# The last turns of a four-stage pipeline in another order, and the last expert layer in input halves

## The chip, the cores and the metric

The kernel runs on one core of a Trainium2 chip. The metric is the device time of one execution in microseconds; the time before is the median of three runs, 785.86 us (784.04 to 786.75). Engines are named as in the profile: PE (matrix products), DVE (vector), ACT (scalar, activation functions), POOL (GpSimd), SP (its queue issues the direct transfers).

## The reference, cut to what matters

Two layer blocks over x (2 x 2048 x 512, float32), each made of an attention-like part and a feed-forward part, all added to x after a layer norm without weights:

```python
x = x + relu(relu(relu(LN(x) @ Wq + bq) @ kp.T) / sqrt(512) + mask) @ vp)   # kp, vp from ctx (2 x 128 x 512)
x = x + dequant(quant6(LN(x))) @ dequant(quant6(W)).T + bias                # blocks of 32, FP6 grid
x = x + LN(x) @ W1.T + mean(ctx @ W2.T) + b                                 # the "mix"
n = LN(x)                                                                   # 16 experts, each takes the
p = softmax(n @ Wg + bg, over the sequence)                                 # 128 tokens of highest p
x[tokens] += (relu(relu(tok @ w1 + b1) @ w2 + b2) @ w3 + b3) * p            # for every expert
```

## The kernel before

Every product is made in three passes of float32r matmuls, from a high part and a rest (names with _h and _l): high x high, high x low, low x high. The high part is made by ACT (hi), the rest by DVE or POOL (lo).

**Phase 1** takes the 32 tiles of 128 tokens (N = 32) through four stages in a loop of turns k = 0 to 35 (LAST = N + 3). It is written out by hand, in one order for each engine; semaphores join them. In turn k a tile k is quantised and its result turned (t2), tile k-1 goes through the feed-forward product (ffn), tile k-2 is turned (t3) and mixed (mix), tile k-3 gets its second residual (x3), its norm for the experts (xn) and its gate logits (lt). Beside these, every fourth turn makes the scores of four tiles (scores; group 7, the last, in turn 27) and gathers logits (logit_rows, in turn 31 for group 6), and up to turn 26 each turn makes one chunk of q (q_chunk) for a later group. From turn 24 on no new tile of x is turned any more; tile 31 is quantised in turn 31, mixed in turn 33.

In an ordinary late turn PE does: t3(k-2), ffn(k-1), attend(k+1), t2(k), mix(k-2). t2(k) waits for xd(k), which POOL writes (L1625) after DVE's q (L1322). DVE does in order: x3(k-3) (L1293), which waits for the end of mix(k-3), its sums bn (L1116), the largest values amax, the scales xs, xrec, xrq, and q of tile k; then the rest of x2T (lo3), x2(k-1) (L1343) with sums, x1(k+1) (L1277) with sums, the rest of xdT (lo2). POOL has the reciprocal roots of the variances (rstd: three or so short operations each), the bias additions (L1611, L1631), xd, and the rests q_lo and s_lo. ACT has xc, the high parts, xn (L854), lt and lrow (L1044).

mix(k) accumulates its two halves of 256 output columns together in banks 6 and 7 and needs x3(k-1) read out of them. The scores go to bank 7 too. In turn 33 four matmuls whose result nobody reads (keep_warm) stand ahead of mix(31).

**Between the phases** all engines wait in phase1_over for the last transfers of phase 1. DVE then finds the 128 largest logits per expert (MAX8 and following), and tokens are gathered.

**Phase 2** runs 16 experts, PE without a pause. hidden(e, layer) makes the hidden layers in two pairs of column chunks, outputs(e) the last layer: for both batches b, 12 matmuls each, over the four input chunks d. It waits for the rests of all four (d_hlo 4e+4). After the last hidden layer twelve matmuls without use stand ahead of outputs(15); DVE scales the two results (y, L1504), and POOL adds each to the output by an indirect DMA (L1664).

```python
        pe.wait_ge(sm.a_h, 4 * E - 3)
        keep_warm(12, wh, ps_hid[0])
        outputs(E - 1)
```

Of the kernel before, what the change touches and what calls it, by code (L numbers as in the profile page):

```python
# [34 lines left out]
P = 128  # L35
# [10 lines left out]
def build(nc, io):  # L46
# [22 lines left out]
        a_xn1 a_xc a_xn4 a_hi1 a_hi2 a_hi3 a_q a_s a_l a_seg  # L69
# [5 lines left out]
    XR = 10  # L75
# [90 lines left out]
    xn4 = [place(f"xn4_{i}", [P, D]) for i in range(2)]  # L166
    top[0] = at_cd + 16 * 1024
# [287 lines left out]
    def _(pe):  # L455
# [59 lines left out]
        def scores(g):  # L515
# [4 lines left out]
            if g >= 1:  # L520
                pe.wait_ge(sm.a_s, g)
                pe.wait_ge(sm.a_l, GRP * g - 3)
                pe.wait_ge(sm.d_x3, GRP * g - 3)
            keys = slice(b * KEYS, (b + 1) * KEYS)
            three_passes(pe, ps_s[:, :], [(k_h[:, c, keys], k_l[:, c, keys], q_h[:, c, :], q_l[:, c, :])
# [22 lines left out]
        def mix(j):  # L548
# [27 lines left out]
            for d in range(1, C):  # L576
                low_tokens(d)
                low_weights(d)
                last = high(d)
            last.then_inc(sm.p_c, 1)  # L580

# [148 lines left out]
        for k in range(1, LAST + 1):  # L730
            if valid(k - 2):
                t3(k - 2)
            if valid(k - 1):
                ffn(k - 1)
# [8 lines left out]
            if scores_of(k) is not None:  # L743
                scores(scores_of(k))
# [6 lines left out]
            if valid(k + 1) and ahead(k):  # L751
                attend(k + 1)
# [74 lines left out]

        wh, _ = weights(0)
# [19 lines left out]
    def _(act):  # L848
# [58 lines left out]

        def norm1(j):
# [20 lines left out]
        def s_relu(g):  # L929
# [3 lines left out]
            act.activation(s32[:, :], ps_s[:, :], ACT.Relu, scale=float(D) ** -0.5).then_inc(sm.a_s, 1)  # L933
# [42 lines left out]
        for k in range(LAST + 1):  # L976
            j = k
            if valid(j):
                act.wait_ge(sm.d_st2, j + 1)
                act.wait_ge(sm.d_q8, j)  # L980
                act.activation(xc[:, :], x1[j % 2][:, :], ACT.Identity, bias=mv[1][:, j % 4, 0:1], scale=-1.0)\
                    .then_inc(sm.a_xc, 1)
            if k == 0:
                setup("wcn")
            j = k - 2
            if valid(j):
                act.wait_ge(sm.p_t3, j + 1)
                act.wait_ge(sm.p_c, max(0, j - 1))
                hi(sm.a_hi3, x2T[j % 2][0][:, :, :], in4(ps_ta))
            j = k - 3  # L990
            if valid(j):
# [4 lines left out]
                act.activation(four, both_halves[:, :, HALF:WIDE], ACT.Copy).then_inc(sm.a_l, 1)  # L996
# [11 lines left out]
            j = k - 3  # L1008
            if valid(j):
                if j >= 2:  # L1010
                    act.wait_ge(sem_xn4[j % 2], 16 * (j // 2))
                norm(3, j, x3[j % 2], xn4[j % 2], sm.a_xn4, sm.g_b4)
            g = scores_of(k)
            if g is not None:
# [23 lines left out]
            if g is not None:  # L1038
# [3 lines left out]
                if g >= 2:  # L1042
                    act.wait_ge(sem_seg[g % 2], 16 * (g // 2))
                act.activation(lrow[g % 2][:, :], ps_ta[0:E * GRP, 0:P], ACT.Identity, bias=bg[:, 0:1])\  # L1044
                    .then_inc(sm.a_seg, 1)

# [60 lines left out]
    def _(dve):  # L1107
# [165 lines left out]
        def first_residual(j):  # L1273
# [464 lines left out]
```

## Time and profile before

| | us |
|---|---|
| median of three runs | 785.86 |
| the profiled execution, its own time | 786.94 |
| its span, first to last instruction | 785.1 |
| turn 27 of phase 1 (from 355.4) | 14.4 |
| turns 28, 29 and 30 | 8.9 each |
| turn 31 | 10.9 |
| turns 32 and 33, to the last mix | 12.0 |
| from there to the first MAX8 | 6.3 |

The span is 1.8 us shorter than the execution's own time, which has what lies around it. Times in the trace are from the span's start. A row of the timeline gives an instruction's start and duration, and in brackets how long the engine had been idle before it and which instruction released it. Matmuls are pipelined: the starts tell their rate, the durations overlap.

### The profile page before, as it was taken

The numbers are of one execution on the slowest core, as the hardware profiler recorded it, in microseconds if no ns is written. First come the engines' busy times: TensorE is split into PE (matmuls) and PEld (weight loads), VectorE is DVE, ScalarE is ACT, GpSimd is POOL, SyncE is SP. The second block draws the span as 40 slices with busy tenths as digits, with TensorE's granted clock in tenths as the row PEclk, the third lists the DMA queues.
The fourth block names the chain that finished last, engine by engine and source line by source line (L and its number), as shares of the span: only waits on it lengthen the run. The fifth ranks groups of instructions, "written<-read, shape, count | busy, mean of one in ns | idle before, by whom it ended". The sixth has DMA issues, their size and how long they took to land.

```text
span 785.1 us, 12311 instructions
## 1 busy us (share of the span) xinstructions
PE 697.4 (89%) x4357; PEld 618.3 (79%) x4357; DVE 572.6 (73%) x1016; ACT 377.8 (48%) x554; POOL 433.3 (55%) x596
## 2 busy tenths in 40 slices
PE   6999999999999999998883007999999999999993
PEld 5766888888888888887672006999999999999992
DVE  5787689898888988777875984576666767677741
ACT  5754444544544444342322203656566666665640
POOL 2735788888888888886752603044444333334321
PEclk9999999999999999999997557999999999999998
DMA  8600122222212221111114244278888888777742
GB/s 312 230 28 14 42 95 67 88 66 92 69 56 96 81 83 50 61 54 43 54 56 156 74 167 119 97 225 243 241 245 236 233 243 239 237 219 218 221 64 34
DMA packets 54093, 103.04 MB, mean 131 GB/s; under 512 B 5392, under 2 KB 6672, under 8 KB 54032
## 3 DMA queue, kind: packets, MB, share of 16 engines
q1 hardware_dynamic: 46864, 85.47, 33.1%
q0 software_dynamic: 7168, 16.78, 9.6%
q8 instruction: 35, 0.57, 0.3%
q14 instruction: 26, 0.21, 0.1%
HBM read 76.68 MB, written 25.17 MB: 130 GB/s over the span
## 4 chain that ended last, share of the span: by engine, by line
PE 81%; DVE 10%; POOL 3%; issue 2%; DMA 1%; ACT 1%; SPq 0%; POOLq 0%; DVEq 0%; ACTq 0%
PE bank L250 45%; PE banks L250 13%; PE bank L257 7%; PE banks L560 4%; PE banks L566 4%; PE banks L570 2%; PE banks L571 2%; DVE pack L1384 1%; DVE left L1391 1%; DVE pos L1386 1%; DVE bn L1116 1%; POOL xd L1625 1%; DVE x L1293 1%; ACT xn L854 1%; DVE q L1322 1%
## 5 line engine op out<-in xcount | busy, mean ns | idle before, releaser
L1664 POOL DMA_INDIRECT out<-y,ids x32 | 76.1, 2379 | 173.6 <-DVE y L1504 169.0
L1128 DVE TENSOR_TENSOR w_l<-w_raw,w_h 128x2048 fp32r<-128x2048 f32 x45 | 103.0, 2289 | 31.3 <-ACT w_h L858 31.3
L1079 ACT ACTIVATE h<-bank,b 128x512 f32<-128x512 f32 x64 | 44.0, 687 | 107.4 <-PE bank L250 107.4
L1116 DVE BATCH_NORM_STATS2 bn<-x 128x6 f32<-128x512 f32 x128 | 88.1, 688 | 8.4 <-DMA x<-x 5.1
L858 ACT ACTIVATE w_h<-w_raw 128x2048 fp32r<-128x2048 f32 x48 | 90.6, 1924 | 5.4 <-DMA w_raw<-w 5.4
L1128 DVE TENSOR_TENSOR hT_l<-h,hT_h 128x512 fp32r<-128x512 f32 x64 | 44.2, 691 | 66.9 <-ACT hT_h L1085 66.9
L250 PE MATMUL bank<-hT_h,w_h 128*128 128x256 f32 x256 | 72.4, 283 | 0.0
L250 PE MATMUL bank<-hT_h,w_l 128*128 128x256 f32 x256 | 72.4, 283 | 0.0
L250 PE MATMUL bank<-tokT_l,w_h 128*128 128x256 f32 x256 | 72.4, 283 | 0.0
L250 PE MATMUL bank<-tokT_h,w_h 128*128 128x256 f32 x256 | 72.4, 283 | 0.0
L250 PE MATMUL bank<-hT_l,w_h 128*128 128x256 f32 x256 | 72.4, 283 | 0.0
L250 PE MATMUL bank<-tokT_h,w_l 128*128 128x256 f32 x256 | 72.4, 283 | 0.0
L1540 POOL TENSOR_SCALAR rstd<-mean_var 128x1 f32<-128x1 f32 x122 | 29.2, 239 | 55.7 <-DVE mean_var L1121 51.7
L1653 POOL DMA_INDIRECT tok<-xn,ids x32 | 31.9, 998 | 47.0 <-DVE ids L1474 28.9
L250 PE MATMUL bank<-wf_h,xdT_h 128*128 128x512 f32 x128 | 53.0, 414 | 0.0
L250 PE MATMUL banks<-w_h,hT_h 128*128 128x512 f32 x128 | 51.2, 400 | 0.0
L250 PE MATMUL bank<-wf_h,xdT_l 128*128 128x512 f32 x128 | 50.3, 393 | 0.0
L250 PE MATMUL bank<-wf_l,xdT_h 128*128 128x512 f32 x128 | 50.0, 391 | 0.0
L250 PE MATMUL banks<-w_h,hT_l 128*128 128x512 f32 x128 | 49.9, 390 | 0.0
L250 PE MATMUL banks<-w_l,hT_h 128*128 128x512 f32 x128 | 49.8, 389 | 0.0
L250 PEld LDWEIGHTS bank<-hT_l,w_h 128*128 128x128 f32 x256 | 49.1, 192 | 0.6
L250 PEld LDWEIGHTS bank<-hT_h,w_h 128*128 128x128 f32 x256 | 49.1, 192 | 0.6
(244 smaller groups left out, 2159.2 us busy)
## 6 DMA issues: line engine op xcount, KB each, us to landing
w_raw<-w SPq DMA_DIRECT2D x48, 1024.0 KB, 6.3
x<-x SPq DMA_DIRECT2D x32, 256.0 KB, 2.8
out<-x SPq DMA_DIRECT2D x32, 256.0 KB, 2.0
xn<-xn SPq DMA_DIRECT2D x32, 256.0 KB, 2.0
mask<-mask_t SPq DMA_DIRECT2D x8, 256.0 KB, 3.1
stage<-wk SPq DMA_DIRECT2D x1, 1024.0 KB, 7.8
stage<-wq SPq DMA_DIRECT2D x2, 512.0 KB, 7.8
stage<-wf SPq DMA_DIRECT2D x1, 1024.0 KB, 10.8
```

Of the source, the lines that this page charges most:

```text
L250: last = pe.matmul(out, a, b, start=(n == 0), stop=(n == 3 * len(pairs) - 1))
L257: last = pe.transpose(bank[:, c * P:(c + 1) * P], src[:, c * P:(c + 1) * P], ident[:, :])
L560: last = pe.matmul(both_halves[:, a, 0:WIDE], xh[:, d, :], wc_h[:, d, a, :], start=(d == 0), stop=(d == C - 1))
L566: pe.matmul(both_halves[:, a, 0:HALF], xh[:, d, :], wc_l[:, d, a * HALF:(a + 1) * HALF], start=False, stop=False)
L570: pe.matmul(both_halves[:, 0, 0:WIDE], xl[:, d, :], wc_h[:, d, 0, :], start=False, stop=False)
L858: act.activation(dst, src, ACT.Copy).then_inc(sem, 1)
L1079: act.activation(h32[n % 2][:, :], ps_hid[n % 4][:, :], ACT.Relu, bias=bias)
L1116: dve.bn_stats(bn6[which][:, j % 2, :], src[:, :]).then_inc(sem_bn[which], 1)
L1128: dve.tensor_tensor(dst, src, hi_part, ALU.subtract).then_inc(sem, 1)
L1540: then(pool.tensor_scalar(r[:, 0:1], m[:, 1:2], LN_EPS, None, ALU.add))
L1653: pool.indirect_dma_start(out=tok[e % 2][:, b, :], out_offset=None, in_=io.xn4, in_offset=bass.IndirectOffsetOnAxis(ap=ids[:, r:r + 1], ax ...
L1664: pool.indirect_dma_start(out=out_rows, out_offset=bass.IndirectOffsetOnAxis(ap=ids[:, r:r + 1], axis=0), in_=y[e % 2][b][:, :], in_offset ...
```

## The change

Turns 25 to 35 are called drain turns.

- PE: attend(k+1) stands right behind t3 and ahead of ffn. The scores of group 7 stand at the head of turn 27, ahead of t3, and go to bank 2 (ps_q[0]), so that they do not wait for x3 and lt.
- DVE: where no scores stood in the turn before (quant_first: turns 25, 26, 27, 29, 30, 31), amax to q of tile k stand ahead of x3(k-3). x1(k+1) stands ahead of x2(k-1), with a third x1 buffer. The sums bn and their mean and variance for x3 are left out for tiles 22 to 29.
- ACT: for those tiles it makes the sums instead (sums4: an ACTIVATE Copy and an ACTIVATE Square of 128x512, each with an accumulator); xn of a tile stands a turn later, behind hi3. xn(31) stands behind the last lrow. SP's order is the same.
- POOL: xd and the bias addition stand at the head of the turn, the roots behind them; s_lo of group 7 stands ahead of the mix bias.
- t3(31) stands inside mix(30), after half of its matmuls. mix(31) makes its output halves one after the other in banks 2 and 3 (last_mix), and x3(31) is made in halves. The four idle matmuls ahead of it are gone.
- Phase 2: outputs(15) takes input chunks 0 and 1 of both batches first, then 2 and 3 (last_outputs); the twelve idle matmuls are gone.

```diff
+    SUMMED = range(N - 10, N - 2)
+    def drain(k):
+        return k >= N - 7
+    def scores_first(k):
+        return scores_of(k) is not None and drain(k)
+    def quant_first(k):
+        return drain(k) and scores_of(k - 1) is None
...
         for k in range(1, LAST + 1):
-            if valid(k - 2):
+            if scores_first(k):
+                scores(scores_of(k))
+            if valid(k - 2) and k - 2 != N - 1:
                 t3(k - 2)
+            if valid(k + 1) and ahead(k) and drain(k):
+                attend(k + 1)
             if valid(k - 1):
                 ffn(k - 1)
...
-            if valid(k - 2):
-                if k == LAST - 2:
-                    pe.wait_ge(sm.a_q, N)
-                    keep_warm(4, wq_h, ps_q[0])
+            if valid(k - 2) and k - 2 != N - 1:
                 mix(k - 2)
+            if k - 2 == N - 1:
+                last_mix()
...
+        def last_outputs():
+            e = E - 1
+            wh, wl = weights(when[(e, 2)])
+            for pair in range(2):
+                pe.wait_ge(sm.d_hlo, 4 * e + 3 + pair)
+                for b in range(B):
+                    if pair == 0:
+                        pe.wait_ge(sm.d_y, B * e + b - 1)
+                    t = slice(b * P, (b + 1) * P)
+                    for d in (2 * pair, 2 * pair + 1):
...
-        pe.wait_ge(sm.a_h, 4 * E - 3)
-        keep_warm(12, wh, ps_hid[0])
-        outputs(E - 1)
+        last_outputs()
...
+        def sums4(j):
+            m = mv[3][:, j % slots[3], :]
+            n = j - SUMMED.start
+            act.wait_ge(sm.a_st4, n)
+            act.activation(squares[:, :], x3[j % 2][:, :], ACT.Copy, scale=-1.0 / D, accum_out=m[:, 0:1])\
+                .then_inc(sm.a_sum, 1)
+            act.wait_ge(sm.a_sum, n + 1)
+            act.activation(squares[:, :], x3[j % 2][:, :], ACT.Square, bias=m[:, 0:1], accum_out=m[:, 1:2])\
+                .then_inc(sm.a_st4, 1)
...
         for k in range(LAST + 1):
+            if valid(k) and quant_first(k):
+                largest(k)
+                quantise(k)
+            if k - 2 == N - 1:
+                third_low(N - 1)
             j = k - 3
...
+            if ahead(k) and drain(k) and valid(k + 1):
+                first_residual(k + 1)
...
+            if drain(k):
+                if scores_first(k):
+                    s_lo(scores_of(k))
+                elif valid(k + 1):
+                    rstd_of(1, k + 1, sm.d_st2, sm.g_r2)
+                if valid(k - 2):
+                    mix_bias(k - 2)
+                if valid(k - 2) and k > N - 7:
+                    rstd_of(2, k - 2, sm.d_st3, sm.g_r3)
+                if valid(k - 3):
+                    rstd_of(3, k - 3, sm.d_st4, sm.g_r4)
+                if scores_first(k):
+                    rstd_of(1, k + 1, sm.d_st2, sm.g_r2)
```

The order on PE at the start of turn 27, before. The first row is the end of mix(24), x_1 is x2 of tile 25 (t3), the products with wf are ffn(26); twelve rows of ffn stand before the first product with kT.

```order
L560 MATMUL banks<-wc_wg_h,x2T_0h 128x288 x2
L257 MATMUL bank<-ident,x_1_125 128x128 x4
L250 MATMUL bank<-wf_h,xdT_h 128x512
L250 MATMUL bank<-wf_l,xdT_h 128x512
L250 MATMUL bank<-wf_h,xdT_l 128x512
```

The same place of the changed kernel, from the last three of the twelve score products:

```order
L252 MATMUL bank<-qT_h,kT_h 128x512
L252 MATMUL bank<-qT_l,kT_h 128x512
L252 MATMUL bank<-qT_h,kT_l 128x512
L259 MATMUL bank<-ident,x_1_125 128x128 x4
L252 MATMUL bank<-wf_h,xdT_h 128x512
L252 MATMUL bank<-wf_l,xdT_h 128x512
L252 MATMUL bank<-wf_h,xdT_l 128x512
```

The scores have moved from behind ffn to ahead of t3.

The order on DVE in turn 29, before; x_0_140 is x3 of tile 26, x_0_124 is x2 of tile 28.

```order
L1293 SCALAR_TENSOR_TENSOR x_0_140<-banks,rstd_all_54,x_0_124 128x512
L1116 BN_STATS bn_72<-x_0_140 128x6
L1307 TENSOR_REDUCE amax<-xc 128x16
L1121 BN_AGGR mean_var_68<-bn_72 128x2
L1317 TENSOR_SCALAR xs<-amax,rstd_74 128x16
L1320 RECIPROCAL xrec<-xs 128x16
L1321 TENSOR_SCALAR xrq<-xrec,rstd_74 128x16
L1322 TENSOR_TENSOR q_113<-xc,xrq 128x512
L1128 TENSOR_TENSOR x2T_1l<-bank,x2T_1h 128x512
L1343 TENSOR_TENSOR x_0_124<-bank,x_0_133 128x512
```

And the changed kernel in the same turn:

```order
L1384 TENSOR_REDUCE amax<-xc 128x16
L1394 TENSOR_SCALAR xs<-amax,rstd_74 128x16
L1397 RECIPROCAL xrec<-xs 128x16
L1398 TENSOR_SCALAR xrq<-xrec,rstd_74 128x16
L1399 TENSOR_TENSOR q_113<-xc,xrq 128x512
L1411 SCALAR_TENSOR_TENSOR x_0_140<-banks,rstd_all_54,x_0_124 128x512
L1225 TENSOR_TENSOR x2T_1l<-bank,x2T_1h 128x512
L1376 SCALAR_TENSOR_TENSOR x_0_133<-bank,x_97 128x512
L1213 BN_STATS bn_70<-x_0_133 128x6
L1218 BN_AGGR mean_var_66<-bn_70 128x2
L1495 TENSOR_TENSOR x_0_124<-bank,x_2_144 128x512
```

q no longer stands behind x3, the sums of x3 are gone, and x1(30) with its sums stands ahead of x2(28).

The order on PE from the end of mix(30) (x2T_0) over t3(31) to mix(31) (x2T_1), before:

```order
L560 MATMUL banks<-wc_wg_h,x2T_0h 128x288 x2
L257 MATMUL bank<-ident,x_1_125 128x128 x4
L459 MATMUL bank<-wq_h 128x512 x4
L560 MATMUL banks<-wc_wg_h,x2T_1h 128x288 x2
L566 MATMUL banks<-wc_l,x2T_1h 128x256 x2
```

And after:

```order
L594 MATMUL banks<-wc_wg_h,x2T_0h 128x288 x2
L259 MATMUL bank<-ident,x_1_125 128x128 x4
L604 MATMUL banks<-wc_wg_h,x2T_0l 128x288
L605 MATMUL banks<-wc_wg_h,x2T_0l 128x256
L600 MATMUL banks<-wc_l,x2T_0h 128x256 x2
L594 MATMUL banks<-wc_wg_h,x2T_0h 128x288 x2
L604 MATMUL banks<-wc_wg_h,x2T_0l 128x288
L605 MATMUL banks<-wc_wg_h,x2T_0l 128x256
L600 MATMUL banks<-wc_l,x2T_0h 128x256 x2
L594 MATMUL banks<-wc_wg_h,x2T_0h 128x288 x2
L628 MATMUL bank<-wc_wg_h,x2T_1h 128x288
L629 MATMUL bank<-wc_l,x2T_1h 128x256
```

t3(31) has moved in front of the second half of mix(30), and mix(31) follows with nothing between.

## Rows read from the trace of the kernel before

**Rows 1.** The page: granted TensorE clock in 40 slices of 19.6 us.

```profile
PEclk9999999999999999999997557999999999999998
```

**Rows 2.** Windows: us, busy time (instructions) of PE, PEld, DVE, ACT, POOL, clock, DMA.

```profile
355.50:370.00 14.50, 12.21 (x63) 10.59 (x62) 9.34 (x20) 3.70 (x7) 8.90 (x14) 0.88 0.11 40
370.00:378.90 8.90, 7.55 (x49) 6.58 (x48) 7.59 (x16) 2.85 (x5) 7.00 (x12) 1.00 0.16 59
396.70:407.60 10.90, 8.52 (x47) 7.62 (x46) 6.61 (x15) 2.37 (x5) 5.95 (x9) 0.84 0.14 52
407.60:419.40 11.80, 10.79 (x72) 9.54 (x70) 5.97 (x11) 3.06 (x6) 5.46 (x10) 1.00 0.24 89
419.40:425.70 6.30, 0.30 (x1) 0.11 (x1) 2.76 (x8) 1.29 (x3) 1.13 (x3) 0.79 0.24 88
```

**Rows 3.** Timeline of PE, turns 27 to 33: start, duration, what, idle before.

```profile
355.41 0.60 PE L257 MATMUL bank<-ident,x 128*128 128x128 f32 x4
...
364.35 0.50 PE L250 MATMUL bank<-v_h,s_h 128*128 128x512 f32 x1 [2.29 <-POOL s_l L1557]
...
369.81 0.60 PE L257 MATMUL bank<-ident,x 128*128 128x128 f32 x4
...
375.20 0.65 PE L257 MATMUL bank<-ident,xd 128*128 128x128 f32 x4 [1.35 <-POOL xd L1625]
...
378.70 0.49 PE L257 MATMUL bank<-ident,x 128*128 128x128 f32 x3
...
402.25 0.80 PE L257 MATMUL bank<-ident,xd 128*128 128x128 f32 x4 [2.38 <-POOL xd L1625]
...
407.42 0.60 PE L257 MATMUL bank<-ident,x 128*128 128x128 f32 x4
...
413.95 1.18 PE L459 MATMUL bank<-wq_h 128*128 128x512 f32 x4
416.13 0.53 PE L560 MATMUL banks<-wc_wg_h,x2T_1h 128*128 128x288 f32 x2 [1.00 <-DVE x2T_1l L1128]
```

**Rows 4.** Timeline of DVE in turn 28: x3 after mix, and q.

```profile
370.01 0.75 DVE L1293 SCALAR_TENSOR_TENSOR x<-banks,rstd_all,x 128x512 f32<-128x512 f32 x1 [2.94 <-PE banks L560]
...
372.94 0.69 DVE L1322 TENSOR_TENSOR q<-xc,xrq 128x512 fp8e4<-128x512 f32 x1
```

**Rows 5.** Timeline of POOL in turns 28 and 32.

```profile
373.23 0.54 POOL L1548 TENSOR_SCALAR rstd<-mean_var,rstd_all 128x1 f32<-128x1 f32 x1
373.73 0.29 POOL L1622 TENSOR_SCALAR xs<-xs 128x16 f32<-128x16 f32 x1
374.10 1.05 POOL L1625 TENSOR_TENSOR xd<-q,xs 128x512 f32<-128x512 fp8e4 x1
...
410.36 0.27 POOL L1548 TENSOR_SCALAR rstd<-mean_var,rstd_all 128x1 f32<-128x1 f32 x1
```

**Rows 6.** Timeline of ACT at the end of phase 1 and the top-k.

```profile
422.62 0.81 ACT L854 ACTIVATE xn<-x,rstd,rstd_all 128x512 f32<-128x512 f32 x1 [2.18 <-POOL rstd L1548]
423.34 0.35 ACT L1044 ACTIVATE lrow<-bank,bg_rows 64x128 f32<-64x128 f32 x1
426.75 0.72 ACT L1057 ACTIVATE exps<-seg_logits,negm 128x512 f32<-128x512 f32 x1 [3.06 <-DVE negm L1389]
427.38 0.19 ACT L1057 ACTIVATION_READ_ACCUMULATOR exps<-seg_logits,negm 128x1 f32 x1
```

**Rows 7.** Timeline of the last expert: PE, DVE, POOL.

```profile
764.60 2.91 PE L459 MATMUL bank<-w_h 128*128 128x512 f32 x12
767.35 0.39 PE L250 MATMUL banks<-w_h,hT_h 128*128 128x512 f32 x1
...
766.10 0.69 DVE L1128 TENSOR_TENSOR hT_l<-h,hT_h 128x512 fp32r<-128x512 f32 x1 [2.19 <-ACT hT_h L1085]
...
761.84 1.56 POOL L1664 DMA_INDIRECT out<-y,ids  x1 [0.30 <-issue]
...
774.08 1.56 POOL L1664 DMA_INDIRECT out<-y,ids  x1 [1.16 <-DVE y L1504]
```

More of the change, by code:

```diff
@@ L576, in mix @@
             for d in range(1, C):
+                if d == 2 and j == N - 2:
+                    t3(N - 1)
                 low_tokens(d)
@@ L580, in mix, with last_mix @@
             last.then_inc(sm.p_c, 1)
+        def last_mix():
+            j = N - 1
+            pe.wait_ge(sm.d_lo3, j + 1)
+            pe.wait_ge(sm.a_q, N)
+            pe.wait_ge(sm.a_s, G)
+            xh, xl = x2T[j % 2]
+            for a in range(2):
+                wide, half = ps_q[a][:, 0:WIDE], ps_q[a][:, 0:HALF]
+                for d in range(C):
+                    pe.matmul(wide, xh[:, d, :], wc_h[:, d, a, :], start=(d == 0), stop=False)
+                    pe.matmul(half, xh[:, d, :], wc_l[:, d, a * HALF:(a + 1) * HALF], start=False, stop=False)
+                    if a == 0:
+                        last = pe.matmul(wide, xl[:, d, :], wc_h[:, d, a, :], start=False, stop=(d == C - 1))
+                    else:
+                        last = pe.matmul(half, xl[:, d, :], wc_h[:, d, a, 0:HALF], start=False, stop=(d == C - 1))
+                last.then_inc((sm.p_ch, sm.p_c)[a], 1)
         def logit_rows(g):
@@ L742, in _ @@
                 t1(k + 9)
-            if scores_of(k) is not None:
+            if scores_of(k) is not None and not scores_first(k):
                 scores(scores_of(k))
@@ L750, in _ @@
                 mean_columns()
-            if valid(k + 1) and ahead(k):
+            if valid(k + 1) and ahead(k) and not drain(k):
                 attend(k + 1)
@@ L989, in _ @@
                 hi(sm.a_hi3, x2T[j % 2][0][:, :, :], in4(ps_ta))
+            if drain(k) and SUMMED.start <= k - 4 < N - 1:
+                norm4(k - 4)
             j = k - 3
@@ L1007, in _ @@
                 hi1(j)
[L1008 to L1012, printed above, removed]
+            if valid(k - 3) and not drain(k):
+                norm4(k - 3)
             g = scores_of(k)
-            if g is not None:
+            if g is not None and not scores_first(k):
                 s_relu(g)
@@ L1045, in _ @@
                     .then_inc(sm.a_seg, 1)
+        norm4(N - 1)
         phase1_over(act)
@@ new lines, in last_residual @@
+        def last_residual():
+            j = N - 1
+            dve.wait_ge(sm.p_ch, 1)
+            dve.wait_ge(sm.g_x2b, j + 1)
+            dve.wait_ge(sm.g_r3, j + 1)
+            dve.wait_ge(sem_x3[j % 2], 16 * (j // 2))
+            dve.wait_ge(sm.a_xn4, j - 1)
+            stats4_done(dve, j - 1)
+            for a in range(2):
+                half = slice(a * HALF, (a + 1) * HALF)
+                if a == 1:
+                    dve.wait_ge(sm.p_c, j + 1)
+                x = dve.scalar_tensor_tensor(x3[j % 2][:, half], ps_q[a][:, 0:HALF], r_all[0][:, j:j + 1],
+                                             x2[j % 2][:, half], ALU.mult, ALU.add)
+                if a == 0:
+                    then(x)
+                else:
+                    x.then_inc(sm.d_x3, 1)
+                    dve.wait_ge(sm.d_x3, j + 1)
+                dve.bn_stats(bn6[3][:, a, :], x3[j % 2][:, half]).then_inc(sem_bn[3], 1)
+                bn_count[3] += 1
+            dve.wait_ge(sem_bn[3], bn_count[3])
+            dve.bn_aggr(mv[3][:, j % slots[3], :], bn6[3][:, :, :].rearrange("p a n -> p (a n)"))\
+                .then_inc(sm.d_st4, 1)
@@ L1352, in _ @@
                 setup("cbcol")
-            if ahead(k) and valid(k + 1):
+            if ahead(k) and not drain(k) and valid(k + 1):
                 first_residual(k + 1)
             g = scores_of(k)
-            if g is not None:
+            if g is not None and not scores_first(k):
                 s_mask(g)
```

159 lines of the change are left out of this document (106 added, 53 removed).

## The prediction

> **What bounds the kernel now.** I read the page's clock line first, then windows cut at the turns, then the timeline of PE, DVE, POOL and ACT in turns 27 to 33, and at last the timeline of the last expert. The clock line is below its 9 in the slices from 412 to 491 us, which are the end of phase 1 and the top-k, where PE has little or nothing to do, and in the last slice [rows 1]. Averages over a slice hide the drain, so the windows matter more: turn 27 has 12.21 us of PE work in 14.50 at a mean clock of 0.88, turn 28 has 7.55 in 8.90 at 1.00 (turns 29 and 30 are alike), turn 31 has 8.52 in 10.90 at 0.84 [rows 2]. Up to turn 26 PE has no gap at all, and in phase 2 neither; there only fewer or faster matmuls would help, and the change makes none. So what can be won lies in four waits: attend(28) for s_l, 2.29 us; t2(k) for xd, 1.35 us in each of turns 28 to 30; the same wait in turn 31, 2.38 us; and from the end of t3(31) at 413.95 to mix(31) at 416.13, four matmuls without use and then 1.00 us of nothing [rows 3]. A fifth place is the last expert: twelve matmuls without use from 764.60 to 767.35 ahead of outputs(15) [rows 7].
>
> The waits of 2.3 and 2.4 us cost twice. In turn 28, from t2 at 375.20 to the next t3 at 378.70, t2 and mix take 3.50 us. In turn 31 the same with one small transpose takes 402.25 to 407.42, 5.17 us, at a clock that fell to the lower of its two levels (1.2 GHz); some 1.5 us are the clock's. In turn 27 attend, transpose and mix take 364.35 to 369.81, 5.46 us, where the pieces at 2.4 GHz make about 3.9: again 1.5. The waits of 1.35 us did not lower it [rows 2, 3].
>
> Why the waits are there: x3 waits for the end of mix and starts at 370.01; in DVE's order q of the next tile stands behind it and its sums, and starts at 372.94; xd on POOL starts at 374.10 and takes 1.05 us; t2 starts at 375.20 and mix behind it [rows 3 to 5]. It is a loop from mix to mix of 8.89 us (369.81 to 378.70).
>
> **The change, part by part.** The sum is made against the profiled execution, 786.94 us, which is 1.08 above the median.
>
> *Turns 28 to 30.* With q ahead of x3 in DVE's order, xd no longer hangs on the mix of its own round (in turn 28 it still does: there the old order stays, but xd then ends about 4.1 us into the turn, when PE has just done t3, attend and ffn). What is left is the work of each engine. PE: 7.55 us. DVE: 7.59, less 0.69 for bn and 0.17 for its aggregate, some 6.7 and 7.1 with the waits between dependent instructions. POOL: 7.00 in twelve instructions, and about eight of them follow another with 0.08 between, as xs and xd do (373.73 plus 0.29 to 374.10): 7.64 [rows 2, 5]. POOL becomes the longest by a hair, and I take 7.64 for a turn. ACT had 2.85 and gets two ACTIVATEs with accumulator; the nearest is the exponential of the same shape, 0.72 and 0.19 for the read, 0.82 from start to end [rows 6]. That makes 4.5 of 7.64, and the pair, which starts when x3 and lt are done (about 2.5 to 3.8 us into the turn), ends as late as 5.7, some 1 us after t2. It then delays the high part of xd; the rest on DVE ends at 7.0 and q of the next tile, behind it, about 1.6 us into the next turn, when POOL is still busy with its rstd until about 2.8: covered, by 1 us. Gain 3 x 1.25 = 3.75 us. Bounds: 3 x (8.89 - 7.55) = 4.0 above, nothing below.
>
> *Turn 31.* No attend here, so PE is free for t2 after 3.2 us; by POOL's clockwork xd comes where it comes in the turns before, 7.64 - 3.50 = 4.14 us in. A wait of 0.9 us instead of 2.38, shorter than the 1.35 that left the clock alone. Then 3.6 us to the end: 7.74 instead of 10.92, gain 3.2 (bounds 1.7 if the clock falls all the same, 4.1 if xd is early).
>
> *Turn 27.* The scores at its head give s_relu, mask and s_l some 3.5 us of cover: scores end at 2.75, s_relu and the mask at about 4.6, s_l's first part at 5.5, and attend(28) stands behind t3, ffn and t2, at 6.4. So 2.29 and the 1.5 of the clock go. Against that stands a new wait: the scores need the last q_lo, which POOL makes at the end of turn 26, where it has 7.64 + 1.3 us to do and starts its round about 1 us into the turn. It ends at about 10.2, PE is there at 10.0: 0.2 us lost (bounds 0 and 1.3, its whole duration as that of a bias addition). Behind the scores everything of PE is queued. Gain 3.6.
>
> *Turns 25 and 26* have a q chunk too, PE is full in them and stays so: nothing.
>
> *Turns 32 and 33.* t3(31) needs x2(31), done 0.8 us before half of mix(30) is through; high and rest of x2T(31) are made under the other half. mix(31) follows without a gap: 416.13 - 413.95 = 2.18 us [rows 3]. Its 24 matmuls stay 24. It needs no x3(30), since it has banks of its own.
>
> *The end of phase 1.* Behind the last matmul x3 and its sums are half as wide, 0.75 + 0.69 become an estimated 0.43 + 0.43: 0.6 won [rows 2, 4]. Two things take it back. lt(31) waits on ACT behind xn(30); and lrow now goes ahead of xn(31), but SP's order is unchanged, so the transfer of the logits stands behind that of xn(31), which starts 0.3 after lrow instead of 0.72 ahead of it [rows 6]. On my count the first MAX8 comes 0.1 later after the last mix than the 6.3 us of before [rows 2]. Loss 0.1 (bounds: 0.6 won, 0.7 lost).
>
> *The last expert.* The first half of outputs(15) needs the rests of chunks 0 and 1, made 2.9 us ahead of the others; it starts at 764.60 in place of the idle matmuls. Its 12 matmuls take 2.75 us, to 767.35, and the second rest ends at 766.79: no wait. The second add started 6.73 us after outputs did (774.08 - 767.35), so now at 771.33; but the first one is ready only 6 matmuls, 1.37 us, earlier, and two adds are 1.56 + 0.30 = 1.86 apart on POOL: 769.96 + 1.86 = 771.82. Gain 774.08 - 771.82 = 2.25 us [rows 7]. PE has no pause here, so the missing idle matmuls cost no clock. Bounds 0 and 2.75.
>
> Sum: 3.75 + 3.2 + 3.6 + 2.2 - 0.1 + 2.25 = 14.9 us. 786.94 - 14.9 = 772.0, and by the median 785.86 - 14.9 = **771.0 us**. Top-k and experts start earlier but are not otherwise touched.
>
> On the clock: a wait of 2.29 us ended at the lower level, one of 1.35 did not [rows 3]. The Trainium skill (TensorE: Matmul & The Clock Gate, "What's actually happening") says that the throttled level is the default and that activity releases it, which speaks against taking sixteen filler matmuls away. By it alone, with the clock down in mix(31) and in outputs(15), those would take up to twice as long. By the rows both places are now filled with real matmuls, and the sum needs nothing for it.
>
> **The rivals.** *POOL holds the turns back.* POOL's last rstd operation took 0.54 us at 373.23, while DVE made q (372.94, 0.69), and 0.27 at 410.36, when DVE had none such [rows 4, 5]. The new order lets q fall on other POOL work. If in each of turns 28 to 31 POOL lost a further 0.69, that is 2.8 us: 773.8. For it: POOL is already the longest. Against it: q ran against POOL before too, and that is in the 7.00. The Trainium skill (SBUF — State Buffer, "Who interferes with whom") has it that a vector instruction with two SBUF inputs blocks a GpSimd instruction that reads SBUF, which is what the 0.54 looks like.
>
> *The loop closes elsewhere.* ACT's pair or xn behind POOL's rstd makes hi2 so late that lo2, then q, then xd come as late as before. Turns 28 to 30 would keep 8.9, turn 31 only lose the clock's 1.5: 3.75 + 1.7 less gain, 776.5. Against it is the 1 us of cover above; for it, that I could not see the accumulating Square in this trace.
>
> *The clock falls once more,* in turn 31 or at the head of turn 27: 1.5 back, 772.5.
>
> *The last layer was not bounding:* if the adds end where their transfers let them, 2.25 back, 773.3. Against it: the first pair of adds, 1.86 apart, shows no pile-up.
>
> *Slower than before.* One mechanism could do it: the clock at 1.2 GHz through the drain. PE has 7.55 us of work per turn, which would become up to twice that; with two turns it has eaten the 14.9, from the third on the kernel is slower (four turns: about 16 above, 787 + 14). It would need waits over 1.35 us in turn after turn, as 2.3 us brought it down; where I find waits, they are of 0.2 to 0.9.
>
> **How the numbers follow.** Forecast 0.62, with its own range of 769.3 to 773 (the bounds of the small terms); POOL 0.15; loop 0.08; clock once 0.08; last layer 0.03; slower 0.04. 769 to 776.5 takes in all but the slower case and part of the loop's tail and of the upper bounds. A measurement of this kernel can tell about 0.3%, 2.4 us, from no change: all cases but the last are beyond it. Faster 0.94, same 0.02, slower 0.04.
>
> **What would show it.** Right: t3 to t3 of 7.6 to 7.7 in turns 28 to 30 with a wait before t2 of 0.3 or less; turn 27 of 10.5 to 10.8 with no wait at attend(28); turn 31 near 7.7 at clock 1.00; mix(31) directly behind mix(30); 6.3 to 6.5 from the last mix to MAX8; outputs(15) from the last hidden matmul on and adds 1.86 apart. Wrong: turns of 8.3 or more with POOL never idle (POOL), or with ACT's Square ahead of a late xdT_h (loop); a mean clock under 1.00 in turns 27 to 33; PE waiting at the scores for q_lo by a whole microsecond or more.

## The result and the profile after

The changed kernel takes 773.78 us (median of four runs, 773.16 to 774.38) against 785.87 (four runs, 784.04 to 786.75): ratio 0.9849, 95% interval 0.9831 to 0.9868, or 12.1 us faster. Its profiled execution took 773.16 us with a span of 771.4; that of before took 786.94. Between the two traces 13.8 us went away, some 1.7 more than between the medians, since the profile of before was 1.1 above its median and that of after 0.6 below.

Windows of the changed kernel: turns 27, 28 and 31, the last two mixes, and from there to the first MAX8 (us, then busy time and instructions of PE, PEld, DVE, ACT, POOL, the granted clock, DMA share and GB/s).

```profile
355.24:365.79 10.55, 10.46 (x63) 8.99 (x62) 7.53 (x16) 4.54 (x11) 7.47 (x13) 1.00 0.13 50
365.79:373.62 7.83, 7.53 (x49) 6.57 (x48) 7.36 (x15) 4.51 (x10) 5.43 (x10) 1.00 0.21 74
388.81:397.36 8.55, 7.63 (x48) 6.17 (x46) 6.97 (x14) 3.79 (x9) 7.12 (x14) 1.00 0.17 62
397.36:407.10 9.74, 9.74 (x70) 9.10 (x68) 6.24 (x11) 4.36 (x10) 6.59 (x14) 1.00 0.30 111
407.10:413.90 6.80, 0.65 (x3) 0.15 (x2) 2.23 (x8) 2.05 (x5) 1.22 (x4) 0.69 0.34 123
```

Against [rows 2] the clock is 1.00 through the whole drain, where turns 27 and 31 had 0.88 and 0.84, and PE's work in the two mixes has no gap. The last window starts inside the last matmul; x3(31), which waits for that matmul, starts at 407.37 (419.43 before). The timeline of PE shows the waits that are left:

```profile
370.12 0.66 PE L259 MATMUL bank<-ident,xd 128*128 128x128 f32 x4 [0.30 <-POOL xd L1785]
373.62 0.60 PE L259 MATMUL bank<-ident,x 128*128 128x128 f32 x4
...
389.92 0.50 PE L252 MATMUL bank<-wf_h,xdT_h 128*128 128x512 f32 x1 [0.50 <-DVE xdT_l L1225]
...
393.27 0.66 PE L259 MATMUL bank<-ident,xd 128*128 128x128 f32 x4 [0.30 <-POOL xd L1785]
394.05 0.27 PE L640 MATMUL bank<-ident,lg_t 128*64 128x128 f32 x1
```

Beside the waits of 2.29, 1.35 and 2.38 us in [rows 3] these are small. The turns, from t3 to t3 (turn 27 together with what stands ahead of it, from t2(26) to t3 of turn 28), and the span from t3(30), which opens turn 32, to the first MAX8:

| us | turn 27 and before | 28 | 29 | 30 | 31 | to MAX8 |
|---|---|---|---|---|---|---|
| before | 17.84 | 8.89 | 8.89 | 8.88 | 10.95 | 18.33 |
| changed | 13.99 | 7.83 | 7.66 | 7.53 | 8.55 | 16.60 |

The last expert on POOL answers to [rows 7]: the two adds are 1.86 us apart, and the last one starts at 760.05. The clock stays at 1.00 in outputs(15) (751.50 to 757.30), as it does in mix(31), with no idle matmuls ahead of either.

```profile
758.19 1.55 POOL L1837 DMA_INDIRECT out<-y,ids  x1 [6.61 <-DVE y L1656]
760.05 1.55 POOL L1837 DMA_INDIRECT out<-y,ids  x1 [0.30 <-issue]
```

### The profile page after: what moved, and what is told of

Read it like the earlier page. It is cut to its first block, busy times and chain, and to the rows that moved or that the text cites. A ratio compares the mean times of both kernels' runs of the same rounds, so it can differ in the third digit from the quotient of the medians.

```text
span 771.4 us, 12297 instructions
## 1 busy us (share of the span) xinstructions
PE 690.9 (90%) x4341; PEld 612.3 (79%) x4341; DVE 569.0 (74%) x1002; ACT 387.9 (50%) x587; POOL 430.1 (56%) x596
## 4 chain that ended last, share of the span: by engine, by line
PE 45%; DMA 19%; issue 18%; DVE 11%; POOL 4%; ACT 2%; POOLq 0%; DVEq 0%; SPq 0%; ACTq 0%
PE bank L252 24%; DMA out<-y,ids 18%; PE bank L259 5%; PE banks L594 3%; PE banks L600 3%; PE banks L252 2%; PE banks L604 2%; PE banks L605 2%; DVE pack L1536 1%; DVE left L1543 1%; DVE pos L1538 1%; DVE bn L1213 1%; POOL xd L1785 1%; ACT xn L926 1%; POOL x L1791 0%
## 5 line engine op out<-in xcount | busy, mean ns | idle before, releaser
L1213 DVE BATCH_NORM_STATS2 bn<-x 128x6 f32<-128x512 f32 x119 | 81.8, 688 | 7.7 <-DMA x<-x 4.7
L1699 POOL TENSOR_SCALAR rstd<-mean_var 128x1 f32<-128x1 f32 x114 | 27.0, 236 | 47.2 <-DVE mean_var L1218 41.5
L252 PEld LDWEIGHTS bank<-tokT_h,w_h 128*128 128x128 f32 x256 | 49.1, 192 | 0.1
L252 PEld LDWEIGHTS bank<-tokT_l,w_h 128*128 128x128 f32 x256 | 49.1, 192 | 0.0
L252 PEld LDWEIGHTS bank<-tokT_h,w_l 128*128 128x128 f32 x256 | 49.1, 192 | 0.0
```

Of the source, the lines that this page charges most:

```text
L252: last = pe.matmul(out, a, b, start=(n == 0), stop=(n == 3 * len(pairs) - 1))
L1213: dve.bn_stats(bn6[which][:, j % 2, :], src[:, :]).then_inc(sem_bn[which], 1)
L1699: then(pool.tensor_scalar(r[:, 0:1], m[:, 1:2], LN_EPS, None, ALU.add))
```

## The experiments

Ratios are to the kernel before, run on the same chip in the same series. Its median was 787.11 us in the first series (tail_only to after_again), 787.49 in the second (q_behind to t3_late) and 785.76 in the third. The changed kernel itself ran again in the first series only (after_again), so the runs of the other two are compared with it by their ratios, 0.9849 and 0.9841.

**tail_only**, the last expert layer alone.

```diff
...
-        keep_warm(12, wh, ps_hid[0])
-        outputs(E - 1)
+        last_outputs()
```

> The kernel before with the new order of the last expert layer alone. Theory: the last add starts 2.2 us earlier, and what follows it grows by about 0.3 as in the changed kernel, so 785.9 - 1.9 = 784.0 us (ratio 0.9975), in the trace adds 1.86 apart and outputs(15) from the last hidden matmul on. Rival, the part behind the last add takes it back or the missing idle matmuls cost clock: 785.5 to 786, ratio 1.000.

Measured: 785.35 us (782.38 to 787.83), ratio 0.9989 (0.9973 to 1.0005), which by itself can't be told from nothing. In the trace the last add stands 346.14 us behind the first MAX8 (772.09 - 425.95) instead of 348.33 (774.08 - 425.75): 2.2 earlier, and the span ends 11.31 us behind it instead of 11.02, as expected.

**drain_only**, the changed kernel with the old last expert layer.

> The changed kernel with the old last expert layer (twelve idle matmuls, then outputs(15) batch by batch). If the two parts add up: 773.8 + 1.9 = 775.7 us, 10.1 under the kernel before. Rival, the two parts share a gain (an earlier phase 2 meets something else, such as a weight transfer): the drain alone then gives clearly more or less than 12.1 less what the last layer alone gives.

Measured: 775.71 us (775.28 to 776.42), ratio 0.9872 (0.9851 to 0.9893). The changed kernel in the same series took 773.22 (below), all of its runs under all of these. So the last layer is worth 2.5 us on top of the drain, and the drain alone is worth 11.4 (787.11 - 775.71). With the 1.8 us of tail_only (787.11 - 785.35) the parts give 13.2 of 13.9: they add up within the spread.

**before_warm**, the kernel before with idle matmuls in its two long waits.

```diff
+            if k == N - 1:
+                keep_warm(8, wq_h, ps_q[0])
             if valid(k):
                 t2(k)
+            if k == N - 5:
+                pe.wait_ge(sm.a_q, N)
+                keep_warm(8, wq_h, ps_q[0])
```

> The kernel before with eight idle matmuls put into each of its two long waits (ahead of attend(28) in turn 27 and ahead of t2(31) in turn 31); nothing else differs. Theory, that each of these waits costs a further 1.5 us because the clock is at its lower level behind it: turn 27 takes 12.9 instead of 14.4 us, turn 31 9.4 instead of 10.9, in all 3.0 us less, 782.9 us (ratio 0.9962), the granted clock 1.00 in both. Rival, the longer stretch behind the waits has another cause, or the fillers delay the real matmuls as much: 785.9, ratio 1.000, turns as long as before.

Measured: 784.71 us (783.71 to 785.92), ratio 0.9979 (0.9965 to 0.9993). Its PE in turn 27:

```profile
361.87 0.60 PE L257 MATMUL bank<-ident,xd 128*128 128x128 f32 x4
362.23 2.10 PE L459 MATMUL bank<-wq_h 128*128 128x512 f32 x8
364.76 0.50 PE L250 MATMUL bank<-v_h,s_h 128*128 128x512 f32 x1 [0.43 <-POOL s_l L1562]
```

The fillers took the place of the wait: attend(28) starts 8.94 us into the turn with them as without (364.76 - 355.82; 364.35 - 355.41). From there to the end of the turn it is 3.93 us instead of 5.46. Turn 31 in the same way ends 3.62 instead of 5.17 us after its t2. That is 1.5 us each, at a clock of 1.00 in both turns, and the first MAX8 comes 3.1 us earlier after t3 of turn 27. The clock's part of each long wait is shown in the trace; the median moved by 2.4 us (787.11 - 784.71) of the 3.0 expected.

**after_again**, the changed kernel once more.

> The changed kernel as it is, for its spread on the same chip as the others: 773.8 us, ratio 0.985. Turn lengths within 0.1 us of the first trace, 7.83, 7.66, 7.53 and 8.55 for turns 28 to 31; rival: if the 1.19 us of one logit part on DVE in turn 30 was a chance meeting, it is 0.23 here and turn 31 takes 7.9 us.

Measured: 773.22 us (772.85 to 773.62), ratio 0.9841 (0.982 to 0.9862). Turns 7.84, 7.66, 7.55 and 8.55: the same to 0.02 us. The long logit operation, 1.19 us on DVE in turn 30 (last section), comes again: it is no chance.

**q_behind**, q again behind x3 on DVE in all turns.

```diff
     def quant_first(k):
-        return drain(k) and scores_of(k - 1) is None
+        return False
```

> The changed kernel with q again behind x3 in DVE's order in every turn; the sums stay on ACT, everything else as changed. Theory A (from turn 28, which kept that order in the changed kernel and still took only 7.83 us): taking x3's sums off DVE is what opened the loop, and the order is worth 0.2 to 0.3 us a turn. Turns 29 and 30 then take 7.8, in all 0.5 us more than the changed kernel, ratio to the kernel before 0.985. Theory B, the prediction's own: q behind x3 closes the loop from mix to mix again, 8.9 less the 0.86 of the sums, 8.0 us or more in turns 28 to 31, 1.5 to 4 us more in all, ratio 0.986 to 0.989.

Measured: 784.05 us (781.91 to 785.63), ratio 0.996 (0.9945 to 0.9974). Against the changed kernel that is 9 us more by the ratios, well beyond theory B's upper end: nearly all of the drain's gain is gone. The runs fall into two groups, three of 781.9 to 782.5 us and six of 784.0 to 785.6, and the trace is of the one at 781.91. Turns 28 to 31 take 8.11, 9.02, 9.01 and 9.53 us, and turn 27 with what stands ahead 19.05, with 1.54 us at the scores for the last q_lo and 2.14 before t2. DVE in turn 29:

```profile
380.21 0.75 DVE L1411 SCALAR_TENSOR_TENSOR x<-banks,rstd_all,x 128x512 f32<-128x512 f32 x1 [1.84 <-issue]
...
382.41 0.69 DVE L1399 TENSOR_TENSOR q<-xc,xrq 128x512 fp8e4<-128x512 f32 x1
```

And POOL around it:

```profile
377.76 1.29 POOL L1771 TENSOR_TENSOR x<-x,mix_bias 128x512 f32<-128x512 f32 x1
379.13 0.22 POOL L1699 TENSOR_SCALAR rstd<-mean_var 128x1 f32<-128x1 f32 x1
379.44 0.58 POOL L1701 TENSOR_TENSOR rstd_all<-rstd,minus_half 128x1 f32<-128x1 f32 x1
...
383.25 1.05 POOL L1785 TENSOR_TENSOR xd<-q,xs 128x512 f32<-128x512 fp8e4 x1 [1.06 <-issue]
384.25 1.29 POOL L1791 TENSOR_TENSOR x<-x,ffn_bias 128x512 f32<-128x512 f32 x1
...
386.79 1.29 POOL L1771 TENSOR_TENSOR x<-x,mix_bias 128x512 f32<-128x512 f32 x1
388.15 0.22 POOL L1699 TENSOR_SCALAR rstd<-mean_var 128x1 f32<-128x1 f32 x1
388.46 0.57 POOL L1701 TENSOR_TENSOR rstd_all<-rstd,minus_half 128x1 f32<-128x1 f32 x1
```

x3 no longer waits for the end of mix (378.83) but for rstd_all, which POOL ends at 380.02 and which the new order puts behind xd, the bias additions and another root. The loop is now q (382.41), xd, ffn bias, mix bias, root (389.03), x3, q: 9.0 us, from 380.02 to 389.03. Theory A, that taking the sums off DVE did most of it, is wrong. Turn 28 is short with the old order of q in both kernels, 7.83 and 8.11 us; why it is, when the turns behind it take 9.0, was not tested by itself.

**sums_dve**, x3's sums back on DVE.

```diff
-    SUMMED = range(N - 10, N - 2)
+    SUMMED = range(N - 10, N - 10)
```

> The changed kernel with x3's sums back on DVE for tiles 22 to 29 (BN_STATS and aggregate, behind x3), ACT's two operations gone; q stays ahead of x3. If DVE's work then bounds the turn: about 6.7 + 0.86 and 0.4 of waits between, 8.0 us a turn in turns 28 to 31 instead of 7.5 to 7.8, 1.6 us more in all, ratio 0.986. If POOL goes on bounding it: turns as in the changed kernel, ratio 0.984.

Measured: 778.72 us (777.80 to 780.52), ratio 0.9893 (0.9874 to 0.9912), some 4 us slower than the changed kernel by the ratios: more than either case. But it isn't in turns 29 and 30, which take 7.71 and 7.72: DVE is now without an idle row in them, and in turn 30 POOL waits 0.41 us for it, so it bounds them, but hardly above POOL's own round. It is where DVE has something besides: turn 27 with what stands ahead 15.09 us (1.14 of them at the scores for q_lo), turn 28 8.55, turn 31 10.97. In turn 31 PE waits 1.66 us for lo2 and 1.41 for the rest of x2T, and DVE twice needs over a microsecond for a small logit operation:

```profile
391.07 1.20 DVE L1355 TENSOR_TENSOR lg_sum<-lt 128x128 f32<-128x128 f32 x1
392.30 0.22 DVE L1356 TENSOR_TENSOR lg<-lg_sum,rstd_all 128x64 f32<-128x64 f32 x1
...
397.22 1.24 DVE L1367 TENSOR_TENSOR lg_t<-lg,rstd_all 128x64 f32<-128x64 f32 x1
```

**scores_late**, the scores of group 7 behind ffn(26) on PE, all other engines as changed.

```diff
-            if scores_first(k):
-                scores(scores_of(k))
             if valid(k - 2) and k - 2 != N - 1:
                 t3(k - 2)
...
-            if scores_of(k) is not None and not scores_first(k):
+            if scores_of(k) is not None:
                 scores(scores_of(k))
```

> The changed kernel with the scores of group 7 back behind ffn(26) on PE alone; the other engines keep the changed order. Theory: attend(28) waits for s_l again, 2.3 us or more (POOL's mix bias stands behind s_lo, so it may get late as well), and the clock falls behind it, 1.5 us: turn 27 takes 14.4 instead of 10.55, 3.8 us more in all, ratio 0.989. Rival, a wait without the clock's part: turn 27 of 12.9, ratio 0.987.

Measured: 778.08 us (777.84 to 778.90), ratio 0.9884 (0.9865 to 0.9903). Turn 27 with what stands ahead takes 17.39 instead of 13.99 us, 3.4 more: PE waits 1.97 us for s_l, and attend to mix behind it take 5.46 us at a mean clock of 0.69, to the digit what they took before (364.35 to 369.81). The window:

```profile
363.72:369.18 5.46, 5.46 (x29) 5.25 (x29) 3.67 (x8) 2.40 (x7) 4.77 (x10) 0.69 0.27 99
```

The rest of this trace's time is elsewhere: the last add stands 297.81 us behind the first of seven idle matmuls that open the experts on PE (L492), 295.31 in that of the changed kernel, and the clock rose later there (last section). The traced execution took 778.90 us, the other three 777.84 to 778.26.

**t3_late**, t3(31) behind mix(30).

```diff
-                if d == 2 and j == N - 2:
-                    t3(N - 1)
...
-            if valid(k - 2) and k - 2 != N - 1:
+            if valid(k - 2):
                 t3(k - 2)
```

> The changed kernel with t3(31) behind mix(30) instead of inside it, no idle matmuls; mix(31) in halves as changed. Theory: PE waits from the end of t3(31) for the high part and the rest of x2T(31), 2.2 us as before, in all 2.2 us more, ratio 0.987, with mix(31) at the full clock. Rival: behind a gap of 2.2 us without fillers the clock is at its lower level in mix(31), which then takes about 1.5 us longer, as the pieces behind the waits of 2.3 us did in the kernel before: 3.7 us more, ratio 0.989.

Measured: 775.61 us (774.74 to 776.55), ratio 0.9853 (0.9836 to 0.987). By its ratio it can't be told from the changed kernel. In the trace it is 18.37 us from t3(30) to MAX8, 1.8 more than in the changed kernel, with one wait:

```profile
404.17 0.60 PE L259 MATMUL bank<-ident,x 128*128 128x128 f32 x4
406.18 0.40 PE L626 MATMUL bank<-wc_wg_h,x2T_1h 128*128 128x288 f32 x1 [1.41 <-DVE x2T_1l L1223]
```

The clock stays at 1.00 behind it, so four idle matmuls are not needed for a wait of this length. But the wait is 1.41 us and not the 2.2 that was expected: the rival, a clock that falls behind a gap of 2.2, was not put to the test.

**pool_old**, POOL's old order with q ahead of x3 (and the sums on DVE). POOL's loop is that of before, with s_lo of group 7 ahead of the last root.

```diff
-    SUMMED = range(N - 10, N - 2)
+    SUMMED = range(N - 10, N - 10)
...
-            if valid(k) and k <= N - 7:
+            if valid(k):
                 rstd_of(1, k, sm.d_st2, sm.g_r2)
-            if valid(k - 2) and k != 2 and not drain(k):
+            if valid(k - 2) and k != 2:
                 mix_bias(k - 2)
-            if valid(k - 3) and not drain(k):
+            if valid(k - 3):
                 rstd_of(3, k - 3, sm.d_st4, sm.g_r4)
...
```

> The changed kernel with POOL's old order (the roots and the mix bias ahead of xd) and, since that order can't wait for sums made late in the turn, x3's sums on DVE again; q stays ahead of x3 on DVE. Beside sums_dve it shows what POOL's order is worth. Theory: xd stands behind the root of x3, which stands behind x3's sums, so the loop from mix to mix is closed over x3, bn, root, xd instead of x3, q, xd; counted along the rows of before it comes some 0.6 us earlier than there: turns 29 and 30 of 8.3 us, against 7.7 in sums_dve and 8.9 before, ratio near 0.991. Rival, POOL's order doesn't matter once q is ahead of x3: turns of 7.7, ratio 0.989 as in sums_dve.

Measured: 793.03 us (791.43 to 793.47), ratio 1.0084 (1.0069 to 1.0099): slower than the kernel before. Turns 28 to 31 take 8.90, 12.50, 8.25 and 12.06 us. Both cases were wrong. DVE's scales need the root of x1, which the old order makes late, behind the root of x2 (in turn 29 DVE is idle for 1.07 us ahead of them, and then held for 1.19); x3 with its sums stands behind q on DVE, and POOL, in order, waits for those sums ahead of xd:

```profile
388.20 0.21 POOL L1699 TENSOR_SCALAR rstd<-mean_var 128x1 f32<-128x1 f32 x1 [3.01 <-DVE mean_var L1218]
388.50 0.57 POOL L1705 TENSOR_TENSOR rstd_all<-rstd,minus_half 128x1 f32<-128x1 f32 x1
389.17 0.27 POOL L1707 TENSOR_SCALAR rstd<-mean_var,rstd_all 128x1 f32<-128x1 f32 x1
389.40 0.30 POOL L1782 TENSOR_SCALAR xs<-xs 128x16 f32<-128x16 f32 x1
389.78 1.05 POOL L1785 TENSOR_TENSOR xd<-q,xs 128x512 f32<-128x512 fp8e4 x1
```

Part of the loss is the clock's: behind PE's waits of 2.62, 3.68 and 3.55 us in turns 27, 29 and 31 its mean is 0.57, 0.70 and 0.67. So q first without POOL's order makes it worse than the kernel before, and POOL's order with q behind (q_behind) gives little: the two orders work only together.

**parts_early**, the logit operations of turn 30 between x2(29) and its sums.

```diff
+                if k == N - 2:
+                    logit_parts(parts_of(k))
                 dve.wait_ge(sm.d_x2, j + 1)
                 stats(2, j, x2[j % 2], sm.d_st3)
...
-            if parts_of(k) is not None:
+            if parts_of(k) is not None and k != N - 2:
                 logit_parts(parts_of(k))
```

> The changed kernel with the four small logit operations of turn 30 on DVE between x2(29) and its sums, where POOL makes roots, instead of behind the sums, where POOL adds the mix bias. Theory: none of them is held up (each 0.22 to 0.27 us instead of once 1.19), lo2(30) ends 0.9 us earlier, PE's wait of 0.50 for xdT_l and POOL's of 0.65 for q go, turn 31 takes 7.8 instead of 8.55, in all 0.7 us less than the changed kernel, ratio 0.983. Rival: the long operation only marks work that POOL had ahead of it, and turn 31 stays at 8.5.

Measured: 773.64 us (772.70 to 774.82), ratio 0.9844 (0.9829 to 0.9858). In the trace the mechanism holds: the four operations take 0.48, 0.23, 0.22 and 0.22, PE's wait of 0.50 is gone, t2 comes 3.89 us into turn 31 instead of 4.46, and the turn takes 7.96 us, 0.6 less. From t2 to its end it is 4.07, as in the changed kernel (4.09). The total doesn't show it; 0.6 us is within the spread of these runs.

**seg_first**, the last logits sent ahead of xn(31).

```diff
-                sp.wait_ge(sm.a_xn4, j + 1)
-                sp.dma_start(xn4_tiles[j], xn4[j % 2][:, :]).then_inc(sem_xn4[j % 2], 16)
+                if j < N - 1:
+                    sp.wait_ge(sm.a_xn4, j + 1)
+                    sp.dma_start(xn4_tiles[j], xn4[j % 2][:, :]).then_inc(sem_xn4[j % 2], 16)
...
+            if k == LAST:
+                j = N - 1
...
-        phase1_over(dve)
+        phase1_over(dve, top_k=True)
```

> The changed kernel with the last transfer of logits ahead of that of xn(31) in SP's order, and DVE's first MAX8 no longer waiting for the transfers of xn (POOL, which gathers them, still does). Theory: the transfer goes out when lrow is done, 1.0 us earlier, and MAX8 with it, in all 1.0 us less, ratio 0.983. Rival: the top-k's start is not what the rest waits for, or xn's transfer, now last, delays the weights behind it: no change.

Measured: 772.83 us (772.46 to 773.76), ratio 0.9831 (0.9817 to 0.9844). In this one trace the transfer went out at 411.81 but took 2.9 us to land (1.8 in that of the next kernel), and MAX8 came only 0.2 earlier than in the changed kernel, counted from t3 of turn 27. Inconclusive by itself.

**both**, the last two edits.

> Both of the last two edits on the changed kernel. If they are independent: turn 31 of 7.8 us and the first MAX8 1.7 us earlier, 1.7 us less than the changed kernel, ratio 0.982, some 771.8 us where the changed kernel takes 773.5.

Measured: 771.82 us (771.73 to 772.13), ratio 0.9818 (0.9805 to 0.9832), 0.0023 to 0.0031 under the two ratios of the changed kernel, whose intervals touch its own; all five runs lie under all ten of the two edits alone in the same series. They lie under all nine of the changed kernel too, though none of those ran in this series. Turn 31 takes 8.02 us, and the logits land in time:

```profile
410.82 0.54 SPq L469 DMA_DIRECT2D seg_logits<-lrow  x1
411.52 0.47 SPq L473 DMA_DIRECT2D xn<-xn  x1
412.72 0.69 DVE L1544 MAX8 pack<-seg_logits 128x8 f32<-128x512 f32 x1 [2.68 <-DMA seg_logits<-lrow]
```

MAX8 comes 53.71 us after t3 of turn 27, 55.62 in the changed kernel: 1.9 earlier, and 1.0 earlier than with parts_early alone (54.71). By its ratio it is the fastest version tried.

## Why the prediction came out as it did

Forecast 771.0 us with 769 to 776.5; measured 773.8. The sign of every term held, and so did the mechanism, but for what the sums on ACT and DVE's other work are worth (turns 28 to 31 below). The sum was 1.1 us too high in the trace, 2.8 against the medians.

- *Turns 28 to 30*, 3.75 forecast: 8.89, 8.89, 8.88 became 7.83, 7.66, 7.53, together 3.64. POOL has no idle row in turns 29 and 30, as forecast. q_behind and pool_old show that the gain hangs on q ahead of x3 and xd ahead of the roots together; the sums on ACT add only 0.05 to 0.2 in turns 29 and 30, where the prediction took them for part of it. Their worth is in turns 27, 28 and 31.
- *Turn 31*, 3.2 forecast, 2.40 measured. This is the term that was mis-sized. Of the 0.8, t2 came 4.46 us into the turn instead of 4.14 (0.3), and t2 to the end took 4.09 instead of 3.6 (0.5), since the logit transpose behind t2 started 0.78 us after it: DVE's rest of x2T, behind q, x3 and lg_t, was late. The prediction had counted POOL's clockwork and forgot DVE's four logit operations, one of them 1.19 us long. parts_early put them elsewhere and gave 0.6 back, all of it ahead of t2; the 0.5 behind t2 stayed (4.07), so its cause is read from the rows only.
- *Turn 27*, 3.6 forecast: from the end of mix(24) to t3 of turn 28 it took 10.55 instead of 14.40, 3.85. The scores started about 0.25 us after mix(24) was through (355.49 - 355.24; forecast 0.2). The 2.3 us and the clock's 1.5 are confirmed, the one by scores_late (3.4 for both), the other by before_warm.
- *Turns 32 and 33*, 2.2 forecast, 2.0 measured; t3_late lost 1.8 with the same step undone.
- *The end of phase 1*, -0.1 forecast, -0.27 measured: inside its bounds. The transfer's place in SP's order, which the prediction named, was worth 0.2 us at MAX8 in the trace of seg_first and 1.0 in that of both.
- *The last expert*, 2.25 forecast: the last add came 2.24 earlier after MAX8 in the first pair of traces, 2.2 in tail_only. But the transfer behind it ends later: span end minus last add is 11.35 us, and 11.02 before (11.31 in tail_only; 11.0 in drain_only, where the adds are 2.72 apart). In eight of the eleven traces with adds 1.86 apart it is 11.2 to 11.6, in the other three (after_again among them) 10.8 to 11.0, so this loss of some 0.3 is usual and not certain. Against the runs the layer gave 2.5 us (drain_only) and 1.8 (tail_only).
- *The step to the median.* The prediction took its sum off the profiled execution, 786.94, and then the same sum off the median. Part of that sum, the clock's 3.0, is read in one execution. The mean clock in runs of before goes from 0.951 to 0.957, and two at these ends took 788.83 and 784.34 us; and before_warm, with the waits filled, spreads over 2.2 us only (783.71 to 785.92). So it may well be that in some runs one of the long waits leaves the clock alone. That is argued from these numbers, not shown.

*The rivals.* POOL's lock, which gives the measured time almost to the digit (773.8), is not what happened, and the match is chance: turns 29 and 30, without an idle row on POOL, took 7.66 and 7.53, with no row longer by 0.69. While DVE made q, one short operation of POOL took 0.47 us in turn 29 and 0.34 in turn 30 (374.89 and 382.55) instead of 0.19, which is no more than in the turns before (0.54 instead of 0.27). The larger effect went the other way: DVE was held by POOL. The loop did not close in the changed kernel: ACT's two new operations let the high part of xd start 0.95 us behind t2 in turn 29, 0.69 in turn 28, and this was covered, as forecast. The loop closes at once when one half of the reordering is undone. The clock never fell in the drain. Counter to the other rivals, the last layer did bound, and nothing was slower.

## What to carry to other kernels

In a loop of several in-order engines, write down for each engine what stands between its input and the operation that the loop goes through, and move them together: here xd ahead of the roots without q ahead of x3 (q_behind) kept 3 of some 13 us (of which about 2 are the last expert layer's), and q first with POOL's old order (pool_old, with the sums on DVE) was 7 slower than the kernel before. An idle wait of some 2 us on PE may be worth a further 1.5 in clock; fillers there are cheap and tell at once whether it is so. Small vector operations that read only SBUF should not stand where POOL makes a wide elementwise operation.

## What the hardware did that was not expected

**DVE held by POOL.** In the changed kernel on DVE:

```profile
380.16 0.68 DVE L1384 TENSOR_REDUCE amax<-xc 128x16 f32<-128x512 f32 x1
380.88 0.67 DVE L1394 TENSOR_SCALAR xs<-amax,rstd 128x16 f32<-128x16 f32 x1
...
387.68 0.23 DVE L1358 TENSOR_TENSOR lg<-lg,lg_sum 128x64 f32<-128x64 f32 x1
387.94 1.19 DVE L1359 TENSOR_TENSOR lg<-lg,logit_shift 128x64 f32<-128x64 f32 x1
```

And on POOL:

```profile
380.23 1.29 POOL L1771 TENSOR_TENSOR x<-x,mix_bias 128x512 f32<-128x512 f32 x1
...
387.75 1.30 POOL L1771 TENSOR_TENSOR x<-x,mix_bias 128x512 f32<-128x512 f32 x1
```

The first row of DVE's, a reduction with one input, runs through POOL's addition at its usual length. The scales (0.23 in other turns) take 0.67 and end at 381.55, the logit addition (0.23) takes 1.19 and ends at 389.13, both within 0.1 us of the end of POOL's addition (381.52 and 389.05). The rows at 391.07 and 397.22 of sums_dve, 1.20 and 1.24 long, end 0.15 us behind such an addition. The Trainium skill (SBUF — State Buffer, "Who interferes with whom") says that a vector instruction with two SBUF inputs contends with a GpSimd instruction that reads SBUF, and that the one issued later waits for the other; the traces agree, with 0.44 and 0.96 us of waiting, and the scales' operation, whose second input is one number per partition, is held too. POOL's short operations (128x1) held none of these: the three logit rows ahead of the long one, from 387.12 on, kept 0.22 to 0.27 us while such operations ran.

**The length of a wait alone does not tell whether the clock falls.** In scores_late a wait of 1.97 us was followed by 5.46 us at a mean of 0.69. In q_behind PE was busy for 0.69 of 3.80 us, with waits of 2.14 and 0.98, at a clock of 1.00, and the 3.92 us behind them were at 1.00 too:

```profile
363.00:366.80 3.80, 0.69 (x5) 0.42 (x4) 3.28 (x7) 0.82 (x3) 2.75 (x5) 1.00 0.24 89
```

The prediction's reading of [rows 3], that 1.35 us is safe and 2.3 is not, holds for those places, and no limit between them can be taken from it. Nor need it be the same in every execution: the traced execution of q_behind took 781.91 us at a mean clock of 0.957, and six of its nine took 784.0 or more, at 0.954 to 0.955.

**The clock's rise at the experts** came later in the trace of scores_late, and the end with it by 2.5 us. The experts open on PE with seven idle matmuls, at 464.74 in the changed kernel and at 467.96 in scores_late. In stretches of 2 us from 6 us after the first of them, scores_late had the lower level until about 475.96:

```profile
473.96:475.96 2.00, 2.00 (x6) 1.55 (x6) 1.37 (x2) 1.86 (x2) 1.32 (x2) 0.50 0.17 68
475.96:477.96 2.00, 2.00 (x9) 1.67 (x8) 1.44 (x1) 0.53 (x1) 0.57 (x1) 0.61 0.76 184
477.96:479.96 2.00, 2.00 (x19) 2.00 (x18) 0.86 (x1) 0.00 (x0) 0.00 (x0) 1.00 0.25 82
```

The changed kernel had 1.00 from the third such stretch behind its first idle matmul on:

```profile
466.74:468.74 2.00, 1.77 (x8) 0.93 (x6) 0.00 (x0) 0.19 (x1) 1.49 (x2) 0.75 0.67 199
468.74:470.74 2.00, 1.45 (x9) 1.27 (x10) 0.81 (x2) 1.16 (x3) 0.92 (x2) 1.00 0.75 199
```

From that first matmul to the last add it is 297.81 us in the one, 295.31 in the other and 295.23 in after_again. The traced execution of scores_late had a mean clock of 0.952, the other three 0.954 and 0.955, so this may belong to one execution and not to the kernel. Why the clock rose later there was not tried.
